# Rounding against limits per block without scaling, the quantised tensor written by VectorE, GpSimd's sums at fixed places, and three-pass projections, in a fused attention and feed-forward kernel

## The reference, cut to what matters

```python
x = x + attn(cond(x, W, cond_index), Wqkv, bqkv, Wo, bo)   # attention within a sequence
x = x + ffn(gated(x, length, conv_w), weight, bias)
# cond:  einsum('bct,bcd->bdt', x, weights[condition])      mixes the 32 rows of a sequence
# attn:  qkv = x @ Wqkv + bqkv (512 -> 3*128); softmax(q k' / sqrt(128)) v; @ Wo + bo
# gated: y = masked sum of each row over its first `length` columns / length
#        x * sigmoid(conv over the rows of y, 5 taps)
# ffn:   both x and weight are quantised per block of 32 columns:
amax = max(abs(block)); exp = floor(log2(amax)) - 8; scale = 2**exp
q = clip(block / scale, -448, 448).astype(float8_e4m3)      # 3 bits of mantissa
out = (q * scale) @ (qw * scale_w).T + bias                 # rounded to bf16
```

## Time and profile before

| what | value |
|---|---|
| median of 3 runs | 169.82 us (169.04 to 169.82) |
| the profiled execution's own time | 170.97 us |
| its span in the trace | 169.3 us |
| PE busy | 130.5 us (77%) |
| DVE busy | 134.9 us (80%) |
| ACT busy | 65.4 us (39%) |
| POOL busy | 64.6 us (38%) |
| mean granted clock of PE | 0.879 of full speed |

### The profile page before, as it was taken

How to read it: one execution, slowest core, us unless ns; L and a number is a source line. 1 busy time by engine, 2 the same in 40 slices (tenths; PEclk the granted TensorE clock), 3 DMA queues, 4 the chain that set the end, 5 groups by cost and what they waited for, 6 DMA issues and landing times.

```text
span 169.3 us, 2698 instructions
## 1 busy us (share of the span) xinstructions
PE 130.5 (77%) x738; PEld 90.4 (53%) x738; DVE 134.9 (80%) x279; ACT 65.4 (39%) x158; POOL 64.6 (38%) x48
## 2 busy tenths in 40 slices
PE   6902899699679889959994999499929955947492
PEld 2402789586477676647573867376716633323130
DVE  4198299759987989899989797978799699599932
ACT  0110433554552646426451545144523463106321
POOL 5330058005612902580555055505551553254500
PEclk9985559999978999999999699959995996587959
DMA  4979103040400000042016001100110011101033
GB/s 112 330 216 321 41 15 122 4 129 6 129 8 2 0 0 0 12 148 98 4 64 187 9 3 64 62 0 0 66 62 0 0 62 62 46 18 41 25 124 124
DMA packets 9489, 11.49 MB, mean 68 GB/s; under 512 B 3954, under 2 KB 4466, under 8 KB 9474
## 3 DMA queue, kind: packets, MB, share of 16 engines
q1 hardware_dynamic: 7186, 8.62, 15.2%
q10 hardware_dynamic: 2096, 2.64, 4.9%
q0 software_dynamic: 192, 0.05, 0.5%
HBM read 7.12 MB, written 4.19 MB: 67 GB/s over the span
## 4 chain that ended last, share of the span: by engine, by line
PE 65%; issue 13%; DVE 6%; DMA 5%; POOL 3%; ACT 3%; SPq 2%; POOLq 1%; ACTq 0%; DVEq 0%
PE ps_qk L439 17%; PE ps_mix L426 12%; PE ps_wo L498 10%; PE ps_v L450 8%; PE ps_ffn L535 7%; DMA mix_w<-in_L_cond_weights_dram 5%; PE ps_att L481 3%; POOL xq L373 2%; PE ps_ffn L533 2%; PE ps_att L471 2%; DVE inv_g L929 1%; PE ps_v L460 1%; SPq L303 1%; PE ps_tr L517 1%; DVE mix_w L972 1%
## 5 line engine op out<-in xcount | busy, mean ns | idle before, releaser
L373 POOL TENSOR_TENSOR xq<-h_clip,scale 128x1024 bf16<-128x1024 bf16 (+1 forms) x11 | 23.1, 2104 | 55.8 <-DVE h_clip L967 37.3
L439 PE MATMUL ps_qk<-xc,wqkv_f 128*128 128x256 f32 x128 | 33.1, 407 | 0.8 <-ACT xc L648 0.8
L439 PEld LDWEIGHTS ps_qk<-xc,wqkv_f 128*128 128x128 f32 x128 | 26.3, 210 | 9.2 <-issue 5.9
L426 PE MATMUL ps_mix<-mix_w,x_sb 128*128 128x128 f32 x128 | 20.8, 331 | 7.5 <-DMA mix_w<-in_L_cond_weights_dram 7.5
L426 PEld LDWEIGHTS ps_mix<-mix_w,x_sb 128*128 128x128 f32 x128 | 19.7, 242 | 8.0 <-issue 7.9
L656 ACT ACTIVATE h_mag<-h 128x512 bf16<-128x512 f32 x20 | 12.4, 625 | 27.4 <-DVE h L941 27.4
L294 POOL TENSOR_TENSOR result<-ffn_out,x 128x512 f32<-128x512 bf16 x12 | 14.5, 1208 | 20.7 <-ACT ffn_out L715 20.7
L498 PE MATMUL ps_wo<-wo_f,o_t 128*128 128x512 f32 x30 | 19.0, 722 | 1.0 <-ACT o_t L663 1.0
L363 POOL TENSOR_TENSOR xb<-x_sb,bo_row 128x1024 f32<-128x1024 f32 x8 | 19.2, 2397 | 0.0
L950 DVE SCALAR_TENSOR_TENSOR h_sum<-h_mag,h 128x512 f32<-128x512 bf16 x20 | 13.7, 691 | 6.8 <-ACT h_mag L656 5.9
L481 PE MATMUL ps_att<-prob_t,v_sb 128*128 128x128 f32 x32 | 5.9, 311 | 15.9 <-issue 15.9
(11 more groups left out here) (86 smaller groups left out, 198.0 us busy)
## 6 DMA issues: line engine op xcount, KB each, us to landing
out_dram<-result SPq DMA_DIRECT2D x16, 256.0 KB, 2.0
x_sb<-in_x_dram SPq DMA_DIRECT2D x7, 512.0 KB
ffn_w_f<-in_L_ffn_weight_dram ACTq DMA_DIRECT2D x2, 512.0 KB, 8.6
mix_w<-in_L_cond_weights_dram SPq DMA_DIRECT2D x56, 4.0 KB, 1.6
wqkv_f<-in_L_attn_Wqkv_dram ACTq DMA_DIRECT2D x1, 768.0 KB, 5.4
x_sb<-in_x_dram SPq DMA_DIRECT2D x2, 256.0 KB, 6.4
bias_row<-in_L_ffn_bias_dram ACTq DMA_DIRECT2D x1, 256.0 KB, 5.6
bo_row<-in_L_attn_bo_dram ACTq DMA_DIRECT2D x1, 256.0 KB, 7.6
```

The source lines that it names most:

```text
L373: nc.gpsimd.tensor_tensor(xq[:, v % 2, t0:t1].rearrange("p t (n k) -> p (t n) k", k=BLOCK), h_clip[:, v % 2, t0:t1].rearrange("p t (n k) - ...
L426: mm = nc.tensor.matmul(ps_mix[t][:, c, :], x_sb[:, u, t, c * P:(c + 1) * P], mix_w[:, u, t, :], start=True, stop=True)
L439: mm = nc.tensor.matmul(ps_qk[:, which, :], wqkv_f[:, c, which * D:(which + 1) * D], xc[:, u % 2, c, :], start=(c == 0), stop=(c == TC - 1))
```

## The change

Four parts. **Rounding without scaling**: nothing is divided by the scale. From the exponent, one instruction `limits` makes three numbers for each block, the floor of the rounding, the upper and the lower bound, in bf16. `magnitude` reads x itself (times gate and 2**20), in an order with the block's index innermost (a stride of 32 fp32 elements in its source). `floor_step` takes the maximum with the floor, `round_sum` adds it to gate times x (the same strided read), `round_back` subtracts it, `clip_high` and `clip_low` bound it; the result is already at its scale and is `xq`. `scale_value`, `scale_inverse`, `gated_inverse`, `scaled`, `clip` and POOL's `dequantise` are gone. **POOL's places**: `residual(s+1)` waits until `xq` of step s+2 is written, and then `final_sum(s-2, 0)`; `final_sum(s-3, 1)` waits until the softmax's division. **Projections in three passes**: ACT's copy of the mixed tensor is rounded to F32R (`xc_hi`), DVE subtracts it from PSUM (`split_mix_lo` writes `xc_lo`), the weight is split once in the same way, and each projection is hi*hi + lo*hi + hi*lo, 12 products with F32R operands. `mix` of the next unit now waits for `xc_lo`. **DVE's order**: the four `softmax_turn` calls stand first, then the gate's chain, then the quantising with the two splits in it, and `residual_sum(s, 0)` comes after the clipping.

```diff
-            def dequantise(v, t0=0, t1=SUB):
...
             bias_low(0)
-            dequantise(0)
+            residual(0)
+            bias_low(1)
             for s in range(UNITS - 1):
-                residual(s)
-                dequantise(s + 1)
+                if s >= 3:
+                    pool.wait_ge(prob_n_done, s + 1)
+                    final_sum(nc.gpsimd, s - 3, 1)
+                pool.wait_ge(xq_done, SUB * (s + 2))
+                residual(s + 1)
                 if s >= 2:
                     final_sum(nc.gpsimd, s - 2, 0)
-                if s >= 2:
-                    final_sum(nc.gpsimd, s - 2, 1)
-                if s == 0:
-                    bias_low(1)
-            residual(UNITS - 1)
+            pool.wait_ge(prob_n_done, UNITS)
+            final_sum(nc.gpsimd, UNITS - 4, 1)
+            pool.wait_ge(xq_done, SUB * (UNITS + 1))
             final_sum(nc.gpsimd, UNITS - 3, 0)
-            dequantise(UNITS)
             final_sum(nc.gpsimd, UNITS - 3, 1)
-            dequantise(STEPS - 1, 0, 1)
-            dequantise(STEPS - 1, 1, 2)
...
-                    pe.wait_ge(xc_done, SUB * (u - 1) + t + 1)
+                    pe.wait_ge(xc_lo_done, SUB * (u - 1) + t + 1)
...
+            def passes(u):
+                hi, lo = xc_hi[:, u % 2], xc_lo[:, u % 2]
+                return [(a, b, c) for a, b in ((wqkv_hi, hi), (wqkv_lo, hi), (wqkv_hi, lo))
+                        for c in range(TC)]
+            def project_qk(u, which, first=0, last=3):
+                if which == 0 and first == 0:
                     if u == 0:
-                        pe.wait_ge(wqkv_loaded, 16)
+                        pe.wait_ge(wqkv_hi_done, 1)
+                        pe.wait_ge(wqkv_lo_done, 1)
                     else:
                         pe.wait_ge(k_copied, u)
-                    pe.wait_ge(xc_done, SUB * (u + 1))
-                for c in range(TC):
-                    mm = nc.tensor.matmul(ps_qk[:, which, :],
-                                          wqkv_f[:, c, which * D:(which + 1) * D],
-                                          xc[:, u % 2, c, :], start=(c == 0), stop=(c == TC - 1))
-                if which == 1:
+                    pe.wait_ge(xc_hi_done, SUB * (u + 1))
+                steps = passes(u)
+                for n in range(first * TC, last * TC):
+                    w, xt, c = steps[n]
+                    if n == 2 * TC and which == 0:
+                        pe.wait_ge(xc_lo_done, SUB * (u + 1))
+                    mm = nc.tensor.matmul(ps_qk[:, which, :], w[:, c, which * D:(which + 1) * D],
+                                          xt[:, c, :], start=(n == 0), stop=(n == len(steps) - 1))
...
+            def round_wqkv():
+                act.wait_ge(wqkv_loaded, 16)
+                nc.scalar.activation(wqkv_hi[:], wqkv_f[:], ACT.Copy).then_inc(wqkv_hi_done, 1)
...
+                if v < WBLOCKS:
+                    act.wait_ge(ffn_w_loaded[v], 16)
+                    src, by = ffn_w_f[:, SUB * v + t, :], ROUND_GAIN
+                else:
+                    act.wait_ge(gain_done, v - WBLOCKS + 1)
+                    src, by = x2[:, (v - WBLOCKS) % 3, t, :], gain[:, t:t + 1]
+                nc.scalar.activation(h_mag[:, v % 2, t, :].rearrange("p (k n) -> p k n", n=NB),
+                                     src.rearrange("p (n k) -> p k n", k=BLOCK), ACT.Abs,
+                                     scale=by).then_inc(h_mag_done, 1)
...
+            def split_mix_lo(u, t):
+                if u >= 2:
+                    dve.wait_ge(v_done, u - 1)
+                dve.wait_ge(xc_hi_done, SUB * u + t + 1)
+                tok = slice(t * P, (t + 1) * P)
+                nc.vector.tensor_tensor(xc_lo[:, u % 2, :, tok], ps_mix[t][:],
+                                        xc_hi[:, u % 2, :, tok].bitcast(F32), ALU.subtract) \
+                    .then_inc(xc_lo_done, 1)
...
+            def limits(v):
                 dve.wait_ge(amax_e_done, v + 1)
+                if v == 0:
+                    dve.wait_ge(limit_k_done, 3)
+                nc.vector.scalar_tensor_tensor(
+                    out=limit[:].rearrange("p a t n -> p a (t n)"),
+                    in0=amax_e[:].rearrange("p t n -> p (t n)").unsqueeze(1)
+                    .to_broadcast([P, 3, SUB * NB]),
+                    scalar=AMAX_FLOOR,
+                    in1=limit_k[:].unsqueeze(2).to_broadcast([P, 3, SUB * NB]),
+                    op0=ALU.max, op1=ALU.mult).then_inc(limit_done, 1)
...
+            def floor_step(v, t0=0, t1=SUB):
+                dve.wait_ge(limit_done, v + 1)
+                dve.wait_ge(h_mag_done, SUB * v + t1)
+                nc.vector.tensor_tensor(blocks_last(h_floor[:, t0:t1]),
+                                        blocks_last(h_mag[:, v % 2, t0:t1]),
+                                        each_block(0, t0, t1), ALU.max) \
+                    .then_inc(h_floor_done, t1 - t0)
...
+            def round_sum(v, t):
+                dve.wait_ge(h_floor_done, SUB * v + t + 1)
+                if v < WBLOCKS:
+                    src, by = ffn_w_f[:, SUB * v + t, :], 1.0
+                else:
+                    src, by = x2[:, (v - WBLOCKS) % 3, t, :], gate[:, t:t + 1]
+                nc.vector.scalar_tensor_tensor(
+                    out=h_sum[:, t, :].rearrange("p (k n) -> p k n", n=NB),
+                    in0=src.rearrange("p (n k) -> p k n", k=BLOCK), scalar=by,
+                    in1=h_floor[:, t, :].rearrange("p (k n) -> p k n", n=NB),
+                    op0=ALU.mult, op1=ALU.add).then_inc(h_sum_done, 1)
+            def round_back(v, t0=0, t1=SUB):
+                dve.wait_ge(h_sum_done, SUB * v + t1)
+                nc.vector.tensor_tensor(h_round[:, t0:t1], h_sum[:, t0:t1], h_floor[:, t0:t1],
+                                        ALU.subtract).then_inc(h_round_done, t1 - t0)
+            def clip_high(v, t0=0, t1=SUB):
+                dve.wait_ge(h_round_done, SUB * v + t1)
+                nc.vector.tensor_tensor(blocks_last(h_min[:, t0:t1]),
+                                        blocks_last(h_round[:, t0:t1]),
+                                        each_block(1, t0, t1), ALU.min) \
+                    .then_inc(h_min_done, t1 - t0)
+            def clip_low(v, t0=0, t1=SUB):
+                dve.wait_ge(h_min_done, SUB * v + t1)
                 if v >= 2:
...
+                    dve.wait_ge(tr_done, SUB * (v - 1))
+                nc.vector.tensor_tensor(blocks_last(xq[:, v % 2, t0:t1]),
+                                        blocks_last(h_min[:, t0:t1]),
+                                        each_block(2, t0, t1), ALU.max) \
+                    .then_inc(xq_done, t1 - t0)
...
             iotas()
+            split_wqkv_lo()
+            split_mix_lo(0, 0)
+            split_mix_lo(0, 1)
             block_max(0, 0)
...
```

More of the change, by code:

```diff
@@ L448, in project_v @@
                     pe.wait_ge(v_copied, u)
-                for c in range(TC):
-                    mm = nc.tensor.matmul(ps_v[:], wqkv_f[:, c, 2 * D:3 * D], xc[:, u % 2, c, :],
-                                          start=(c == 0), stop=(c == TC - 1))
-                mm.then_inc(v_done, 1)
+                steps = passes(u)
+                for n in range(first * TC, last * TC):
+                    w, xt, c = steps[n]
+                    if n == 2 * TC:
+                        pe.wait_ge(xc_lo_done, SUB * (u + 1))
+                    mm = nc.tensor.matmul(ps_v[:], w[:, c, 2 * D:3 * D], xt[:, c, :],
+                                          start=(n == 0), stop=(n == len(steps) - 1))
@@ L541, in _ @@
             mix(0, 1)
[L542 removed]
+            project_qk(0, 0, 0, 2)
+            project_v(0, 0, 2)
+            project_qk(0, 0, 2, 3)
+            project_v(0, 2, 3)
             project_qk(0, 1)
[L544 removed]
             mix(1, 0)
```

232 lines of the change are left out of this document (92 added, 140 removed).

## The result

The changed kernel took 204.21 us (203.78 to 205.87), the kernel before beside it 169.43: a ratio of 1.208, 95% interval 1.199 to 1.216. The profiled execution took 204.1 us, its span is 202.4. The direction was right, the size was not: 188 was predicted, and the range ended at 204. Some executions come out over 1.5% longer than the fastest of their kernel (two of e3_fp32's four, three of e5_pool's four, one of e9_pool_small's, two of e12_o_first's twelve): the ratios leave them out, and the traces of e5_pool and e9_pool_small are of such ones.

What follows compares the result with a forecast made beforehand. It took a ring to bound the kernel: scores, softmax, late VectorE transposes, attend, output projection. Start +11.9, six units +9.8, tail -3.8 make +17.9 on a 169.3 span, 187.2; adjusted to execution time, 188 us, range 174 to 204.

Steps and rivals of the forecast that it cites:

- The mechanism: In the loop: the 2.3 us stall before attend moves to before the second output projection, 4.15 us, released by x2.
- F32R near the bf16 price: Projections on PE: 12 products at 0.108 us each, 1.30 a projection instead of 1.73, -0.43 three times a unit.
- no row shows such a read; I price it like the dense ones, 0.63 and 0.7: h_mag and h_sum, reading fp32 elements 128 bytes apart, were priced like dense reads: 0.63 and 0.7 us.
- the walk: The whole span link by link: +17.9 us on 169.3; as it stands 180 to 195, with 46 in 100.
- strided reads are slow: Rival, 20 in 100: strided reads cost up to double in ring, start and tail, up to +16 us, 196 to 204.
- Predicted 17.6 with an FFN: One loop unit, from S (start of its scores on PE) to the next scores: 17.6 us, four such units.
- The walk's 0.9 for the slow FFN: Behind the gap in a unit: scores and FFN at the lower clock lose about +0.9 us.
- Without an FFN 16.0 was predicted: The two loop units without an FFN, scores 1 to 3: about 16.0 us each, with only the projection doubled.
- The start: +11.9: Up to the scores of unit 1: 51.8 us against 39.94, with first softmax_inverse at 38.4 instead of 31.44.
- the step "24.9": The tail, from scores 7 to the last transposes: 24.9 us against 28.7, a gain of 3.8.
- The loop's contention, costed at nothing: GpSimd's sums beside VectorE in the loop: 0 us, hidden by VectorE's wait for h_mag; 1.2 us without that cover.
- the ring: The loop's chain of scores, attend, h_mag, rounding, x2, second output projection, next scores sets a unit's time; six units +9.8 us.

Runs made afterwards that it cites:

- e3_fp32: The changed kernel with fp32 projections of 4 products again, without the splits and the rounding of the weight: 200.4 us (196.9 to 202.3), no ratio given.
- e5_pool: The changed kernel with GpSimd's final_sum(s-3, 1) behind the wait for xq instead of the softmax's division: 206.5 us (202.9 to 207.0), no ratio given.
- e9_pool_small: The changed kernel with GpSimd's final sums cut to 32 of 512 columns and one fill of the result tile in the start: 202.7 us, ratio 1.190.
- e12_o_first: The kernel before with the four softmax_turn calls first on VectorE and copy_o ahead of both halves of magnitude on ScalarE: 168.6 us, ratio 0.991.
- e6: The changed kernel with 18 unused products of zeros on TensorE in the gap before the second output projection: 198.1 us, ratio 1.169.
- e1: The changed kernel with dense instead of strided reads in magnitude and round_sum, so the rounding is not the reference's: 193.9 us, ratio 1.153.
- e4: The changed kernel with only the start reordered: weight magnitudes ahead of round_wqkv, maxima, limits and most of the rounding ahead of the splits: 196.3 us, ratio 1.168.
- e11: The whole change reordered: e2 and e4, gate instructions between softmax_turns, magnitudes ahead of copy_o, masked sums ahead of the maxima: 184.3 us, ratio 1.084.
- e2: The changed kernel with residual_sum(s, 0) right behind round_back, ahead of the second split and the clips: 193.5 us, ratio 1.156.
- e7: The changed kernel with four edits together: dense reads, early residual sum, the start's order of before, GpSimd's sum behind xq: 187.0 us, ratio 1.103.
- three edits: Dense reads (e1), early residual sum (e2) and reordered start (e4), each alone on the changed kernel: 193.9, 193.5 and 196.3 us; together in e7.
- a fourth: The edit of e5_pool, GpSimd's final sum behind the wait for xq, added to the changed kernel in e7: 187.0 us with all four.

## Why the prediction was wrong in size

**The mechanism was right.** No gap before `attend`, the gap before the second `ps_wo` released by `x2`, the clock at 0.50 behind it, `h_floor` waiting 2.2 us for `h_mag`, F32R near the bf16 price: all are in the rows above. The tests that would have shown it wrong did not come true: the gap is 5.2 us, not under 2, and the first `prob_inv` comes at 39.20.

**The step that failed first: "no row shows such a read; I price it like the dense ones, 0.63 and 0.7".** Measured: 1.19 and 1.11 us. Undoing it takes 9.3 us off the span (193.1 for 202.4), of the 15.3 by which the walk fell short (33.2 - 17.9). It was the rival "strided reads are slow", with its 196 to 204 and 20 in 100. That the measured 204.2 falls at the rival's upper end is partly luck: it had up to 16 us for the reads (10.8 in six units, 3 in the start, 2 in the tail), they cost 9 to 10 (6.8, 0.5 and 2.5), and the rest are the terms below. The rule of the Trainium skill, SBUF — State Buffer, "Door 1: The DMA port swizzle", pointed that way. The traces agree in direction: 1.19 for 0.72 us on ScalarE, 1.11 for 0.75 on VectorE.

**A unit.** Predicted 17.6 with an FFN, measured 19.1 on average: `x2` came 2.0 us later (h_mag ends at S+9.3 for S+7.7, and the stretch from there is 7.5 for 7.1), and from `x2` to the next scores 2.06 us pass where the walk had 1.8. The walk's 0.9 for the slow FFN has to be looked for on the way to `x2`, and there PE is in fact late for the convolution by up to 1.7 us; how much of it reaches `x2`, no run shows, since e6 gives 1.05 a unit only net of a new contention. Without an FFN 16.0 was predicted and 18.1 measured. In e1, with dense reads, these two units took 17.4 and 16.8, so 2.3 of the loop's error is theirs and not the reads'; what made them longer I did not isolate. One part of the order is not named in the list of the change, though the prediction counted with it: both masked sums now stand behind both maxima, where `masked_sum(s, 0)` stood ahead of them. In these units the masked sums are through at S+3.0 and the convolution starts at S+3.1, where it started at S+2.1 before.

**The start: +11.9 for +13.2.** The first `prob_inv` was 0.8 late, the rest follows behind it with the longer `h_mag` and `h_sum`. That the order is what costs was right (e4, e11).

**The tail: the step "24.9".** It measured 28.85. The walk left out a link: behind the gate's chain it went straight to the last step's two halves, but `h_mag` must come first, and stands behind the copy of the transposed tensor on ScalarE:

```profile
185.56 0.26 DVE L959 SCALAR_TENSOR_TENSOR limit<-amax_e,limit_k 128x96 bf16<-128x96 f32 x1
...
186.82 2.21 ACT L673 ACTIVATE h_mag<-x,gain 128x512 bf16<-128x512 f32 x2
188.07 0.42 DVE L977 TENSOR_TENSOR h_floor<-h_mag,limit 128x512 bf16<-128x512 bf16 x1 [2.25 <-ACT h_mag L673]
```

2.25 us from the limits to the first `h_floor`. The rest, walk and trace: scores to the end of `h_mag` 8.85 and 9.79; from there to the end of the maxima 8.4 and 9.35; GpSimd's hold-up and the gate's chain 2.3 and 1.09; the two last halves with latencies 5.35 and 6.37, most of that the strided `h_sum`. 2.25 + 0.94 + 0.95 - 1.21 + 1.02 is the 3.95 between 24.9 and 28.85. Of the predicted gain of 3.8 us nothing is left; with dense reads (e1) 2.3 is, 26.4 for 28.7.

**The loop's contention, costed at nothing:** near enough for the final sums (1 to 3 us in all, e9), and for a reason close to the one given. What the prediction did not see is how much this hangs on the order of things: in e2, e6, e7 and e11, where other work ends earlier, GpSimd's sums fall on `masked`.

## What to carry to other kernels

Where a change makes an engine read in an order that no row shows, price it from both ends and let the far end stand in the sum if the read is on the ring. Walk the tail instruction by instruction, each wait with what its engine has queued ahead of it. And when a stall goes, ask which link is late next, and by how much: here two removed stalls (before `attend`, and before the first output projection) came back at the next place for a gain of 2% at most, and three edits worth 8 to 11 us alone gave 17 together, with a fourth beside them that held up the residual sum. A test that keeps the clock up also moves everything else: read where the time went before the difference is given to one cause.
